# Mean sweeps of a graph network over 128 runs of the edge list, one run per partition

## The chip, the cores and the metric

One core of a Trainium2 chip runs the kernel; its engines are TensorE (PE), VectorE (DVE), ScalarE (ACT), GpSimd (POOL) and SyncE (SP). The metric is the device time of one execution in microseconds (us). Differences of up to 0.3% are about what a measurement of this kernel can't tell from none.

## The reference, cut to what matters

Four graph layers run over N = 6250 nodes of F = 128 features and E = 106250 edges (`src`, `dst`), which are sorted by `dst`. The last layer takes, twice, the mean of the neighbours' rows and two dense products:

```python
def _mean_aggregate(h, src, dst, num_nodes):
    msgs = h[src]
    summed = jax.ops.segment_sum(msgs, dst, num_segments=num_nodes)
    deg = jax.ops.segment_sum(jnp.ones((src.shape[0],), h.dtype), dst, num_segments=num_nodes)
    return summed / jnp.maximum(deg, 1.0)[:, None]

neigh = _mean_aggregate(x, src, dst, n)
h = jax.nn.relu(x @ W_in[0] + neigh @ W_in[1])
neigh = _mean_aggregate(h, src, dst, n)
return h @ W_out[0] + neigh @ W_out[1]
```

The three layers before it (a maximum over messages, a sum over messages, an attention) aren't touched. All is float32.

## The kernel before, in words

The program is a row of blocks, each with one instruction stream per engine; a block begins when all engines have ended the one before. A preparation block reads the edge list and makes tables: `src_cols` (the source node of each edge, 128 consecutive edges in a column of 128 partitions), marks that tell whether an edge has the same receiver as the one before it (written to memory, `edge_meta`), and for each node the row of its last edge (`end_i`) and one over its degree (`inv_deg`). Constants: T = 832 columns of P = 128 edges (106496 with padding), groups of CT = 4 columns (512 edges), NB = 208 groups, a ring of RING = 8 groups (32 columns), SLOTS = 4.

Stages 1 to 5 are each a sweep over the edges followed by a node phase in the same block. Stages 4 and 5 are the two mean aggregations; their sweep is `mean_phase` (from line 1306), written out without loops:

- POOL issues for each column an indirect DMA (L1321) that gathers 128 rows of 512 bytes of `sender_table`, one for each edge; before a group it waits on `e_pre` until the PE has transposed the group that used that place of the ring.
- The PE transposes the group (L1361), so that features lie on partitions and 512 edges along the row. VectorE runs a scan over them (L1404): sum = mark x sum + row, so a sum starts anew at each new receiver. The PE transposes back (L1371), ScalarE copies from PSUM (L1387), SP stores 256 KB to `scan_rows` (L1334) and counts stored groups in `e_kept`. SP also loads the marks, 1 MB for 8 groups, spread to all partitions (L1329).
- The row of a node's last edge in `scan_rows` then holds its sum.

The node phase (`node_phase`, from line 692) gathers on POOL those rows, 49 indirect DMAs in 13 groups of up to 4 (L746). Groups 0 to 3 wait only until the groups of edges that they need are stored, the others until all are. VectorE multiplies by `inv_deg` (L859), the PE transposes and multiplies (L1039 to L1057), ScalarE copies between (L978, L988), VectorE takes the result (L884), and SP stores it as the next stage's table (L779). The end of stage 4 is where the sweep of stage 5 begins; at the end of stage 5 a layer norm and the output follow. `scan_rows` is stored group-wise: 4 consecutive rows per partition (`"(p c) f -> p c f"`), which the preparation takes into account by permuting `end_i` (lines 611 to 618).

In the preparation, SP loads `dst` and `src` (L316 to L318), one word of each tile (L323), then the weights (L325, L341), and later stores `dst_rows` (L347), reads back each tile's last receiver (L353), after which VectorE counts (L557, L573) where each node begins. ScalarE meanwhile fills `receiver_rows` with zeros (L414), 2 MB each, in pieces of 16 KB that lie 832 rows of 512 bytes apart from partition to partition (line 404), and makes a factor table with the PE (L645, L655).

Of the kernel before, what the change touches and what calls it, by code (L numbers as in the profile page):

```python
# [17 lines left out]
P = 128  # L18
E = 106250
N = 6250  # L20
F = 128
# [19 lines left out]
assert NB % (2 * STRETCH) == 0 and STRETCH * CT * 4 == P  # L41
# [44 lines left out]
def gnn_program(nc, a, out):  # L86
# [14 lines left out]
    with ctx:  # L101
# [30 lines left out]
        end_i = sb("end_i", [P, NT], I32)  # L132
        mask = sb("mask", [P, NT])
# [114 lines left out]
        with ExitStack() as pctx:  # L248
# [23 lines left out]
            lasts, junk = carve("gath", [T]), (carve("gath", [T]), small[:, :, :].rearrange("p a b -> p (a b)")[:, 0:T])  # L272
            node_i = psb("node_i", [P, NT], I32)
# [35 lines left out]
            with nc.Block() as block:  # L309
                @block.sync  # L310
                def _(sp):

                    sp.wait_ge(filled, 3)
                    sp.sem_inc(filled, -3)
# [4 lines left out]
                    with nc.allow_non_contiguous_dma("one word of each tile"):  # L319
                        for c in range(TC):  # L320
                            lo, n = (1, P - 1) if c == 0 else (0, P if c < TC - 1 else rest + 1)
                            first = (c * P + lo - 1) * P
                            sp.dma_start(prev_r[lo:lo + n, c:c + 1],  # L323
                                         a["dst"][first:first + n * P].rearrange("(p k) -> p k", k=P)[:, P - 1:P]).then_inc(loaded, 16)
                    sp.dma_start(wm[:, :, :], a["L1_gnn_Wm"].rearrange("(t p) n -> p t n", p=P)).then_inc(wm_in, 16)  # L325
# [129 lines left out]
                def _(pool):  # L455
                    pool.memset(dst_r[:, TC - 1, :], N).then_inc(filled, 1)
                    pool.memset(src_r[:, TC - 1, :], 0).then_inc(filled, 1)
                    pool.memset(prev_r[:, 1:TC], N).then_inc(p_done, 1)
# [6 lines left out]
                    pool.wait_ge(p_done, 7)  # L465
                    pool.sem_inc(p_done, -7)
# [14 lines left out]
                def _(v):  # L481
# [58 lines left out]
                    chain(v.tensor_copy(head_ofT[:, :], bank[4][0:HEADS, 0:P]))  # L540
                    v.wait_ge(weights_in, 16 * 18)
# [62 lines left out]
                    chain(v.tensor_copy(end_i[:, :], end_f[:, :]))  # L604
                    chain(v.tensor_scalar(node_f[:, :], node_f[:, :], float(EP), None, ALU.add))
# [15 lines left out]
                def _(pe):  # L621
# [12 lines left out]
                    pe.transpose(bank[4][0:HEADS, 0:P], head_of[:, :], ident[:, :]).then_inc(turned, 1)  # L634

# [52 lines left out]
        marks = [over_head[:, :].bitcast(BF16)[:, h * RING * EB:(h + 1) * RING * EB] for h in range(2)]  # L688
# [3 lines left out]
        def node_phase(k):  # L692
# [35 lines left out]
            def gpsimd(pool):  # L728
                def gather(q, s):
                    g = 2 * q + s  # L730
                    if g == 0 or g - 1 in checked:
# [36 lines left out]
                if gathers:  # L768
# [537 lines left out]
        def mean_phase(k):  # L1306

            table, pre_ps, back_ps = send_d, bank[0:2], bank[4:6]
            before, rounds = started["edge"], NB // RING
            base, loads = NB * started["mean"], NB // RING  # L1310
            base_stored, base_marks = 16 * (NB // SLOTS) * started["mean"], 16 * (loads // 2) * started["mean"]

            def gpsimd(pool):
                for i in range(NB):
                    s = i % RING
                    if i >= RING:

                        pool.wait_ge(e_pre, base + i - RING + 1)
                    for c in range(CT):
                        t = i * CT + c  # L1320
                        pool.indirect_dma_start(out=gath[s][:, c, 0:F], out_offset=None, in_=table[:, :],  # L1321
                                                in_offset=bass.IndirectOffsetOnAxis(ap=src_cols[:, t:t + 1], axis=0)).then_inc(gathered[s], 16)

            def sync(sp):
                def load_marks(j):
                    if j >= 2:
# [603 lines left out]
```

## Time and profile before

| what | us |
|---|---|
| three executions | 7039.76, 7061.51, 7058.68 (median 7058.68) |
| profiled execution, its own time | 7064.64 |
| its span, first to last instruction | 7062.7 |
| its mean granted TensorE clock | 0.677 of full speed |

Times in the profile count from the first instruction. A group of instructions shows its busy time, the mean of one, and the idle time of its engine just before it with what ended it; "issue" is time in which the engine waited for nothing that the profile shows, "remote" an end that it can't name, and an engine's name with q is its sequencer. The windows show busy time and instruction count of each engine in a stretch.

### The profile page before, as it was taken

To read this page: it belongs to the slowest core of one execution; us is meant where nothing else is said; L and a number is where in the kernel's file an instruction comes from. 1 tells how busy PE (TensorE), PEld (TensorE's weight loads), DVE (VectorE), ACT (ScalarE), POOL (GpSimd) and SP (SyncE) were. 2 spreads that over 40 slices of the span, in tenths; PEclk is the share of its full clock that TensorE was granted. 3 is DMA by queue.
4 is the path that set the end of the run, shared out by engine and by line. 5 is a ranking of instruction groups with operands and counts; after the bars stand their busy time and mean duration, and the time that the engine had idled before them with its cause. 6 is when DMAs were issued, how large, how long until landed. Compare 5 with 4: busy or idle time off the path is not lost. (4 is left out here: it accounts for less than half of the span.)

```text
span 7062.7 us, 75749 instructions
## 1 busy us (share of the span) xinstructions
PE 3269.4 (46%) x16319; PEld 2442.7 (35%) x16319; DVE 2306.4 (33%) x4133; ACT 1222.9 (17%) x2253; POOL 3621.3 (51%) x3810
## 2 busy tenths in 40 slices
PE   1357777777647885344444443223222332222323
PEld 1334444444436663233333432122222222222222
DVE  4223333332346663233333335222222212222223
ACT  0111111111224442112112211011111111110111
POOL 2355555555440004655555553666666656666664
PEclk7667777777779997666666666555555565555556
DMA  9757767766448984222222222333333323333332
GB/s 266 234 173 223 218 206 214 217 207 211 139 139 295 317 292 99 67 76 78 77 78 77 79 75 68 98 115 117 117 109 116 113 72 116 117 116 115 112 122 73
DMA packets 701309, 1015.77 MB, mean 144 GB/s; under 512 B 151346, under 2 KB 403179, under 8 KB 691147
## 3 DMA queue, kind: packets, MB, share of 16 engines
q1 hardware_dynamic: 379672, 485.85, 21.5%
q0 software_dynamic: 134688, 301.60, 15.5%
q10 hardware_dynamic: 186780, 226.46, 9.4%
q8 instruction: 59, 0.97, 0.1%
q14 instruction: 110, 0.89, 0.0%
HBM read 580.89 MB, written 433.03 MB: 144 GB/s over the span
## 5 line engine op out<-in xcount | busy, mean ns | idle before, releaser
L1321 POOL DMA_INDIRECT gath<-sender_table,src_cols x1664 | 1571.3, 944 | 903.3 <-issue 488.2
L1361 PE MATMUL bank<-ident,gath 128*128 128x128 f32 x1664 | 405.4, 391 | 1739.2 <-issue 1192.5
L1404 DVE TENSOR_TENSOR_SCAN scan<-over_head,scan,bank 128x512 f32<-128x512 bf16 x416 | 532.2, 1279 | 1896.1 <-remote 1488.6
L1594 POOL DMA_INDIRECT gath<-attention_table,src_cols x832 | 796.2, 957 | 663.8 <-POOLq L1591 423.8
L1118 POOL DMA_INDIRECT gath<-joint_table,src_cols x832 | 788.2, 947 | 671.1 <-POOLq L1115 281.1
L1361 PEld LDWEIGHTS bank<-ident,gath 128*128 128x128 f32 x1664 | 278.1, 202 | 1842.0 <-issue 1783.3
L1387 ACT ACTIVATE rows<-bank 128x512 f32<-128x512 f32 x416 | 245.0, 597 | 2186.2 <-remote 1597.5
L1293 DVE TENSOR_TENSOR_SCAN scan<-meta,scan,bank 128x512 f32<-128x512 bf16 x208 | 266.1, 1279 | 835.2 <-DVEq L1290 434.4
L1857 DVE TENSOR_TENSOR_SCAN scan<-bank,scan,hid 128x512 f32<-128x512 f32 x208 | 266.6, 1282 | 643.5 <-DVEq L1856 339.7
L746 POOL DMA_INDIRECT gath<-scan_rows,end_i x147 | 140.0, 952 | 633.7 <-ACTq L1521 560.6
L1371 PE MATMUL bank<-ident,scan 128*128 128x128 f32 x1664 | 385.4, 377 | 1.5 <-DVE scan L1404 0.8
L1194 PE MATMUL bank<-hid,w 128*128 128x512 f32 x416 | 295.6, 802 | 126.7 <-PEq L1193 107.3
L1687 PE MATMUL bank<-ident,scan 128*128 128x128 f32 x832 | 175.8, 350 | 354.8 <-issue 191.0
L1186 PEld LDWEIGHTS bank<-same,recv 128*128 128x128 f32 x1664 | 256.6, 236 | 203.7 <-issue 203.7
L1371 PEld LDWEIGHTS bank<-ident,scan 128*128 128x128 f32 x1664 | 316.0, 205 | 2.4 <-DVE scan L1404 2.4
L1227 ACT ACTIVATE hid<-bank,b 128x512 f32<-128x512 f32 x208 | 143.0, 688 | 949.7 <-ACTq L1226 498.8
L1186 PE MATMUL bank<-same,recv 128*128 128x128 f32 x1664 | 303.7, 338 | 0.0
L1183 PE MATMUL bank<-ident,gath 128*128 128x128 f32 x832 | 166.6, 336 | 279.7 <-issue 142.1
L1184 PE MATMUL bank<-small,w1w 1*128 1x512 f32 x416 | 293.4, 791 | 0.0
L1679 PE MATMUL bank<-small,over_head 128*128 128x128 f32 x1664 | 285.6, 329 | 0.0
L1562 DVE TENSOR_TENSOR_SCAN scan<-bank,scan,hid 128x512 f32<-128x512 f32 x208 | 265.9, 1278 | 39.2 <-issue 14.8
L1679 PEld LDWEIGHTS bank<-small,over_head 128*128 128x128 f32 x1664 | 270.6, 246 | 0.0
(250 smaller groups left out, 5244.6 us busy)
## 6 DMA issues: line engine op xcount, KB each, us to landing
scan_rows<-rows SPq DMA_DIRECT2D x624, 256.0 KB
recv<-receiver_rows SPq DMA_DIRECT2D x416, 256.0 KB
attention_scan_rows<-rows ACTq DMA_DIRECT2D x208, 264.0 KB
receiver_rows<-gath ACTq DMA_DIRECT2D x26, 2048.0 KB
factor_rows<-gath ACTq DMA_DIRECT2D x208, 256.0 KB
scan_rows<-rows ACTq DMA_DIRECT2D x208, 256.0 KB
gath<-factor_rows SPq DMA_DIRECT2D x208, 256.0 KB
over_head<-edge_meta SPq DMA_DIRECT2D x52, 1024.0 KB
```

Of the source, the lines that this page charges most:

```text
L1118: pool.indirect_dma_start(out=landed[s][:, c, 0:width], out_offset=None, in_=table[:, :], in_offset=bass.IndirectOffsetOnAxis(ap=src_cols[ ...
L1184: pe.matmul(b[:, :], w1w[:, :], wrow[r][:, :], start=False, stop=False)
L1186: ins = pe.matmul(b[:, c * P:(c + 1) * P], recv[r][:, c, :], same[s % 2][:, c, :], start=False, stop=c == CT - 1)
L1194: pe.matmul(msg_ps[s % 2][:, :], w2[:, :], hid[s % 2][:, :], start=True, stop=True).then_inc(e_msg, 1)
L1293: chain(v.tensor_tensor_scan(scan[s % 2][:, :], go_on, src, scan[1 - s % 2][:, EB - 1:EB], ALU.add if expands else ALU.mult, ALU.max if ex ...
L1321: pool.indirect_dma_start(out=gath[s][:, c, 0:F], out_offset=None, in_=table[:, :], in_offset=bass.IndirectOffsetOnAxis(ap=src_cols[:, t:t ...
L1361: ins = pe.transpose(b[:, c * P:(c + 1) * P], gath[s][:, c, 0:F], ident[:, :])
L1371: ins = pe.transpose(back_ps[i % 2][:, c * P:(c + 1) * P], scan[i % 2][:, c * P:(c + 1) * P], ident[:, :])
L1404: v.tensor_tensor_scan(scan[i % 2][:, :], go_on, pre_ps[i % 2][:, :], scan[1 - i % 2][:, EB - 1:EB], ALU.mult, ALU.add).then_inc(e_scan, 1)
L1594: pool.indirect_dma_start(out=gath[s][:, c, :], out_offset=None, in_=att_d[:, :], in_offset=bass.IndirectOffsetOnAxis(ap=src_cols[:, t:t + ...
L1679: ins = pe.matmul(fac_ps[s % 2][:, c * P:(c + 1) * P], over_head[:, t * P:(t + 1) * P], factor_c[s // SB][:, :], start=True, stop=True)
L1857: chain(v.tensor_tensor_scan(scan[s % 2][:, :], fac_ps[s % 2][:, :], hid[s % 2][:, :], scan[1 - s % 2][:, EB - 1:EB], ALU.mult, ALU.add))
```

## The change

The edge list is cut into 128 runs of T = 832 consecutive edges, one per partition. Column t of the sweep is then edge t of each run, so that consecutive edges of a run follow each other in one partition, and the sums can be made row by row by VectorE, without transposes: `run_row(t)` = `run_row(t - 1)` x `goes_on[:, t]` + `run_row(t)`, in place in the ring, which has 4 slots of TR = 8 columns. SP stores a slot of 512 KB when it is summed, from each partition 4 KB that are consecutive in `scan_rows`. POOL, before it fills a slot again, waits for the slot's sums and its store.

A receiver whose edges cross the border of two runs is mended at the end: the last rows of all runs are transposed, scanned with `whole_row` (a run that is one single receiver passes its predecessor's sum on) and transposed back; POOL gathers for each run the row at which its first receiver ends (`lead_end`), VectorE adds what the runs before carry over, and POOL scatters the rows back. Only then does it gather for the nodes, all 49 without further waits, by `end_row`, which isn't permuted.

The preparation loads `src_run` and `dst_run` with two DMAs each, the last receiver of the run before each run (`before_run`, one word per partition) with one, and makes `goes_on`, `lead_end` and `whole_row` with some 20 more VectorE instructions and one matmul. ScalarE has nothing to do in the sweeps, and the marks aren't loaded there.

```diff
@@ preparation, SP, behind the loads of one word of each tile (POOL: three more fills and an iota ahead) @@
-                    sp.wait_ge(filled, 3)
+                    sp.wait_ge(filled, 6)
...
+                    runs = E // T
+                    for t, name in ((src_run, "src"), (dst_run, "dst")):
+                        sp.dma_start(t[0:runs, :], a[name][0:runs * T].rearrange("(p t) -> p t", t=T)).then_inc(run_loaded, 16)
+                        sp.dma_start(t[runs:runs + 1, 0:E - runs * T], a[name][runs * T:E].rearrange("(p t) -> p t", p=1)).then_inc(run_loaded, 16)
+                        sp.dma_start(before_run[1:P, :], a["dst"][0:(P - 1) * T].rearrange("(p t) -> p t", t=T)[:, T - 1:T]).then_inc(run_loaded, 16)
...
@@ preparation, VectorE, behind the copy to head_ofT @@
+                    v.wait_ge(run_loaded, 16 * 5)
+                    v.tensor_copy(lead_len[:, :], before_run[:, :]).then_inc(v_done, 1)
+                    v.tensor_copy(start_run[:, :], run_start[:, :]).then_inc(v_done, 1)
+                    v.tensor_copy(dst_flat[:, :], dst_run[:, :]).then_inc(v_done, 1)
+                    v.tensor_tensor(goes_on[:, 1:T], dst_flat[:, 1:T], dst_flat[:, 0:T - 1], ALU.is_equal).then_inc(v_done, 1)
+                    v.tensor_tensor(goes_on[:, 0:1], dst_flat[:, 0:1], lead_len[:, :], ALU.is_equal).then_inc(v_done, 1)
+                    chain(v.tensor_copy(goes_in[:, :], goes_on[:, :]))
+                    chain(v.memset(goes_in[:, 0:1], 1.0))
+                    chain(v.tensor_tensor_scan(dst_flat[:, :], goes_in[:, :], zero_c[:, 0:1].to_broadcast([P, T]), 1.0, ALU.mult, ALU.add))
+                    chain(v.reduce_sum(lead_len[:, :], dst_flat[:, :], mybir.AxisListType.X))
...
+                    v.tensor_copy(whole_all[:, :], lead_len[:, 0:1].to_broadcast([P, P])).then_inc(whole_ready, 1)
+                    v.wait_ge(whole_turned, 1)
+                    chain(v.tensor_copy(whole_row[:, :], bank[2][:, 0:P]))
...
+                    chain(v.tensor_copy(end_row[:, :], end_f[:, :]))
@@ preparation, PE, ahead of the factor table @@
+                    pe.wait_ge(whole_ready, 1)
+                    pe.matmul(bank[2][:, 0:P], whole_all[:, :], ident[:, :], start=True, stop=True).then_inc(whole_turned, 1)
@@ mean_phase, new bodies; all of the old ones goes @@
+            def gpsimd(pool):
+                for t in range(T):
+                    j = t // TR
+                    if t % TR == 0 and j >= SLOTS:
+                        pool.wait_ge(e_scan, summed_before + (j - SLOTS + 1) * TR)
+                        pool.wait_ge(stored[j % SLOTS], stored_before + 16 * (j // SLOTS))
+                    pool.indirect_dma_start(out=run_row(t), out_offset=None, in_=send_d[:, :],
+                                            in_offset=bass.IndirectOffsetOnAxis(ap=src_run[:, t:t + 1], axis=0)).then_inc(gathered[t // CT % RING], 16)
+                for s in range(SLOTS):
+                    pool.wait_ge(stored[s], stored_before + 16 * (RUNS // SLOTS))
+                pool.indirect_dma_start(out=lead_rows[:, :], out_offset=None, in_=scan_d[:, :],
+                                        in_offset=bass.IndirectOffsetOnAxis(ap=lead_end[:, :], axis=0)).then_inc(lead_in, 16)
+                pool.wait_ge(lead_summed, m + 1)
+                pool.indirect_dma_start(out=scan_d[:, :], out_offset=bass.IndirectOffsetOnAxis(ap=lead_end[:, :], axis=0),
+                                        in_=lead_rows[:, :], in_offset=None).then_inc(lead_out, 16)
+                pool.wait_ge(lead_out, 16 * (m + 1))
+            def sync(sp):
+                for j in range(RUNS):
+                    sp.wait_ge(e_scan, summed_before + (j + 1) * TR - 1)
+                    sp.dma_start(by_run[:, j * TR:(j + 1) * TR, :], run_rows[j % SLOTS]).then_inc(stored[j % SLOTS], 16)
+            def tensor(pe):
+                pe.wait_ge(e_scan, summed_before + T - 1)
+                pe.transpose(bank[0][:, 0:P], run_row(T - 1), ident[:, :]).then_inc(last_turned, 1)
+                pe.wait_ge(carries_made, m + 1)
+                pe.transpose(bank[1][:, 0:P], carries[:, 0:P], ident[:, :]).then_inc(carries_turned, 1)
+            def vector(v):
...
+                for t in range(T):
+                    if t % CT == 0:
+                        v.wait_ge(gathered[t // CT % RING], gathered_before + 16 * CT * (t // (CT * RING) + 1))
+                    if t > 1:
+                        v.wait_ge(e_scan, summed_before + t - 1)
+                    if t > 0:
+                        v.scalar_tensor_tensor(run_row(t), run_row(t - 1), goes_on[:, t:t + 1], run_row(t), ALU.mult, ALU.add).then_inc(e_scan, 1)
+                v.wait_ge(e_scan, summed_before + T - 1)
+                v.wait_ge(last_turned, m + 1)
+                v.tensor_tensor_scan(carries[:, 1:P + 1], whole_row[:, :], bank[0][:, 0:P], 0.0, ALU.mult, ALU.add).then_inc(carries_made, 1)
+                v.wait_ge(lead_in, 16 * (m + 1))
+                v.wait_ge(carries_turned, m + 1)
+                v.scalar_tensor_tensor(lead_rows[:, :], bank[1][:, 0:P], goes_on[:, 0:1], lead_rows[:, :], ALU.mult, ALU.add).then_inc(lead_summed, 1)
@@ node_phase, POOL @@
-                    if g == 0 or g - 1 in checked:
+                    if k <= 3 and (g == 0 or g - 1 in checked):
...
-                                                in_offset=bass.IndirectOffsetOnAxis(ap=end_i[:, t:t + 1], axis=0)).then_inc(node_got[g], 16)
+                                                in_offset=bass.IndirectOffsetOnAxis(ap=(end_i if k <= 3 else end_row)[:, t:t + 1], axis=0)).then_inc(node_got[g], 16)
```

## Rows read from the trace of the kernel before

**Rows 1.** The page: span, and two of its costliest groups
```profile
span 7062.7 us, 75749 instructions
...
L1321 POOL DMA_INDIRECT gath<-sender_table,src_cols x1664 | 1571.3, 944 | 903.3 <-issue 488.2
...
L1404 DVE TENSOR_TENSOR_SCAN scan<-over_head,scan,bank 128x512 f32<-128x512 bf16 x416 | 532.2, 1279 | 1896.1 <-remote 1488.6
```

**Rows 2.** Windows: preparation, sweep 4, its node phase, sweep 5, its node phase
```profile
core 0: us, PE busy (x) PEld busy (x) DVE busy (x) ACT busy (x) POOL busy (x), PEclk, DMA share, GB/s
0.00:262.60 262.60, 42.18 (x173) 35.01 (x173) 102.67 (x298) 15.83 (x27) 58.60 (x67) 0.71 0.94 274
...
4436.00:5616.40 1180.40, 334.95 (x1624) 284.23 (x1624) 258.44 (x202) 117.86 (x200) 785.62 (x832) 0.56 0.35 114
5616.40:5745.50 129.10, 54.21 (x239) 35.65 (x239) 24.75 (x32) 27.12 (x47) 46.81 (x50) 0.75 0.22 67
5745.50:6926.30 1180.80, 337.48 (x1624) 286.92 (x1624) 259.45 (x203) 118.18 (x201) 785.65 (x832) 0.56 0.35 114
6926.30:7062.70 136.40, 56.19 (x239) 35.94 (x239) 54.04 (x192) 21.92 (x46) 46.68 (x49) 0.71 0.21 64
```

**Rows 3.** Timeline where sweep 4 begins: start, duration, engine, line, idle before
```profile
4436.03 0.94 POOL L1321 DMA_INDIRECT gath<-sender_table,src_cols  x1 [61.29 <-POOLq L1867]
...
4439.78 0.94 POOL L1321 DMA_INDIRECT gath<-sender_table,src_cols  x1 [0.30 <-issue]
...
4443.51 0.90 PE L1361 MATMUL bank<-ident,gath 128*128 128x128 f32 x3 [9.60 <-DMA gath<-sender_table,src_cols]
```

**Rows 4.** Line L1321 alone: what ended POOL's idle time before it
```profile
  issue: 488.2, 1583
  remote: 251.1, 64
```

**Rows 5.** Timeline of a stall in sweep 4
```profile
4499.33 1.28 DVE L1404 TENSOR_TENSOR_SCAN scan<-over_head,scan,bank 128x512 f32<-128x512 bf16 x1 [21.15 <-remote]
...
4500.76 0.66 PE L1361 MATMUL bank<-ident,gath 128*128 128x128 f32 x2 [20.49 <-issue]
...
4510.77 0.94 POOL L1321 DMA_INDIRECT gath<-sender_table,src_cols  x1 [5.12 <-remote]
```

**Rows 6.** Groups by form, VectorE: the added operation, factor from SBUF, and without
```profile
L1841 DVE SCALAR_TENSOR_TENSOR small<-small,carried 128x128 f32<-128x128 f32 x26 | 9.1, 352 | 5.1 <-DVEq L1840 3.8 <-issue 1.1 <-DVE sum_carry L1838 0.2
...
L1812 DVE SCALAR_TENSOR_TENSOR small<-max_c,small 128x128 f32<-128x128 f32 x26 | 7.6, 292 | 3.9 <-issue 0.9 <-DVEq L1811 0.5
```

**Rows 7.** Timeline, node phase of stage 4: a gather begun under a VectorE instruction
```profile
5663.10 0.69 DVE L859 TENSOR_TENSOR recv<-gath,inv_deg 128x512 f32<-128x512 f32 x1 [0.44 <-DVE recv L884]
5663.25 1.36 POOL L746 DMA_INDIRECT gath<-scan_rows,end_i  x1 [0.30 <-issue]
```

**Rows 8.** Timeline, node phase of stage 4, from the last copy to the next sweep
```profile
5648.45 0.60 ACT L1387 ACTIVATE rows<-bank 128x512 f32<-128x512 f32 x1 [0.78 <-PE bank L1371]
...
5651.91 0.94 POOL L746 DMA_INDIRECT gath<-scan_rows,end_i  x1 [15.55 <-SPq L1339]
...
5692.39 0.95 POOL L746 DMA_INDIRECT gath<-scan_rows,end_i  x1 [0.30 <-issue]
5697.13 0.60 ACT L988 ACTIVATE hid<-bank 128x512 f32<-128x512 f32 x1 [25.27 <-ACTq L984]
...
5731.80 0.29 DVE L859 TENSOR_TENSOR recv<-gath,inv_deg 128x128 f32<-128x128 f32 x1 [0.44 <-DVEq L837]
...
5745.46 0.94 POOL L1321 DMA_INDIRECT gath<-sender_table,src_cols  x1 [52.12 <-POOLq L1867]
```

**Rows 9.** Timeline of the preparation: POOL's fill, SP's word-wise loads, VectorE's first count
```profile
1.28 3.51 POOL L462 MEMSET over_head<- 128x4096 f32 x1
...
16.86 13.44 SPq L323 DMA_DIRECT2D prev_r<-in_dst_dram  x7
...
86.12 1.08 DVE L557 TENSOR_SCALAR_CACHE_REDUCE gath<-gath,node_f 128x832 f32<-128x832 f32 x1 [30.09 <-DVEq L556]
```

More of the change, by code:

```diff
@@ L40 @@
 STRETCH = 8
-assert NB % (2 * STRETCH) == 0 and STRETCH * CT * 4 == P
+TR = 2 * CT
+RUNS = T // TR
+assert RUNS % SLOTS == 0 and T % TR == 0 and NB % (2 * STRETCH) == 0 and STRETCH * CT * 4 == P
 BIG = 3.0e38
@@ L132, in gnn_program @@
         end_i = sb("end_i", [P, NT], I32)
+        end_row = sb("end_row", [P, NT], I32)
+        src_run = sb("src_run", [P, T], I32); goes_on = sb("goes_on", [P, T])
+        whole_row = sb("whole_row", [P, P]); lead_end = sb("lead_end", [P, 1], I32)
         mask = sb("mask", [P, NT])
@@ L686, in gnn_program @@
         t_exp_p = sem("t_exp_p")
-        marks = [over_head[:, :].bitcast(BF16)[:, h * RING * EB:(h + 1) * RING * EB] for h in range(2)]
+        run_rows = [gath_flat[:, s * TR * F:(s + 1) * TR * F].rearrange("p (c f) -> p c f", f=F) for s in range(SLOTS)]
+        lead_rows, carries = prod[0][:, 0:F], prod[1][:, 0:P + 1]
+        lead_in, lead_out = rank_in
+        lead_summed, last_turned, carries_made, carries_turned = factor_out[0:4]
         started = {"node": 0, "scatter": 0, "firsts": 0, "edge": 0, "mean": 0}
@@ L767, in gpsimd @@
                                                 in_offset=bass.IndirectOffsetOnAxis(ap=first_dst[:, c:c + 1], axis=0)).then_inc(firsts_got, 16)
-                if gathers:
+                if 1 <= k <= 3:
                     pool.sem_inc(e_kept, -NB)
@@ L1306, in mean_phase @@
         def mean_phase(k):
[L1308 to L1311, printed above, removed]
-            def gpsimd(pool):
[L1314 to L1322, printed above, removed]
@@ L1324, in sync @@
-            def sync(sp):
-                def load_marks(j):
-                    if j >= 2:
-                        sp.wait_ge(e_scan, base + (j - 1) * RING)
-                    sp.dma_start(marks[j % 2], meta_d[0, j * RING * EB:(j + 1) * RING * EB].partition_broadcast(P)).then_inc(meta_in[j % 2], 16)
-                def store(i):
-                    sp.wait_ge(e_rows, base + i + 1)
-                    sp.dma_start(scan_d[i * EB:(i + 1) * EB, :].rearrange("(p c) f -> p c f", c=CT), rows_flat[i % SLOTS][:, :, :]).then_inc(stored[i % SLOTS], 16)
-                def kept(i):
-                    sp.wait_ge(stored[i % SLOTS], base_stored + 16 * (i // SLOTS + 1))
-                    sp.sem_inc(e_kept, 1)
-                load_marks(0)
-                load_marks(1)
-                for i in range(NB):
-                    store(i)
-                    if i >= 2:
-                        kept(i - 2)
-                    if i % RING == RING - 1 and i // RING + 2 < loads:
-                        load_marks(i // RING + 2)
-                kept(NB - 2)
-                kept(NB - 1)
@@ L1381, in scalar @@
[L1381 to L1404 removed]
+            m = started["mean"]
```

80 lines of the change are left out of this document (40 added, 40 removed).

## The prediction

> **What bounds the kernel now.** I read three things in order: the page for where the changed line stands, the windows by stage for how long each stage lasts, and the timeline inside a stage for what ends last there. The page puts POOL first by busy time at the mean sweeps' gather line, L1321, with VectorE's scan L1404 far behind it [rows 1]. In the windows the two sweeps last 1180.4 and 1180.8 us, and POOL works 785.6 us in each on its 832 gathers; PE, VectorE, ScalarE and the DMA engines (0.35) are all far from full [rows 2]. So one wants to know why 832 gathers take 1180 us. At the start of a sweep they go out 1.250 us apart (three gaps between 4436.03 and 4439.78), 0.94 of work and 0.30 until the next [rows 3]. 832 x 1.250 = 1040 us. The other 140 us a sweep are stalls: L1321's idle time splits into 488.2 us of those 0.30 gaps and 251.1 us ended by "remote" in only 64 places [rows 4].
>
> The stall can be seen in the timeline of the first sweep. Scan, copy and transposes stand still for some 21 us (VectorE 21.15, PE 20.49) while POOL goes on; POOL itself then waits 5.12 us at 4510.77 [rows 5]. It waits for `e_pre`, that is for the PE to have transposed the group that holds the ring's next place: 32 rows of 1.250 us are 40 us of cover, and the chain gather, transpose, scan, transpose back, copy eats it. It is not the gathered data that are late: a group's first transpose starts at 4443.51, 2.8 us after its last gather's issue ended at 4440.72 [rows 3]. I read the stall as the PE round trip's, since VectorE and ScalarE resume together and the PE after them. Why the PE is slow in answering, no row says.
>
> **The change, part by part.** *Sweeps, gathers.* They are as many, 832 a sweep, of the same form, so 1040 us is the floor and POOL remains the bound. What changes is who frees the ring. A slot of 8 rows is free when it is summed and stored; POOL asks at row 8j for slot j-4, whose last gather went out 25 gathers, 31 us, earlier. It needs: landing 2.8 us, sums 2 us, store. For a 256 KB store the rows give 2.9 us from the end of the last copy (5648.45 + 0.60) to POOL's start behind it [rows 8]; I take 4 for 512 KB, bounds 2.9 and 5.8. Together 9 us of 31. That its pieces lie 416 KB apart in memory is no cost that I can see: the preparation's zero fill has the same stride and the stage moves 274 GB/s [rows 2]. So both sweeps lose the stalls: 2 x 140.5 = **-281 us**. Removing the 52 loads of 1 MB marks, the 1664+1664 transposes and 416 copies is worth nothing by itself; they lie beside POOL.
>
> *Sweeps, VectorE.* 831 `scalar_tensor_tensor` of 128x128 replace 208 scans. Such an instruction with its factor read from SBUF takes 352 ns, without 292 [rows 6]. Each waits for the one before; with a tenth of a microsecond for that, 0.45 us a row against 1.250, so VectorE keeps up with a factor of 2.7. Its cost lies elsewhere: it holds up the gathers. At 5663.10 VectorE starts a two-operand instruction that ends at 5663.79, POOL starts a gather at 5663.25, and that gather takes 1.36 instead of 0.945 us [rows 7]: 0.41 more, the 0.54 us left of the other less 0.12. So a gather wants something 0.12 us after its start that such an instruction holds. The sums are active 4 x 0.352 of each 5 us, 28% of the time, and what is left of one when it is hit is 0.176 us on average: 0.05 us a gather, 41 a sweep, **+83 us**. Bounds: 0 if the bursts fall between the gathers' moments, and 0.175 us a gather (every second waits out a whole one), 291 us, if they fall on them. I take random phase, since landing times vary by tenths.
> By the Trainium skill (SBUF - State Buffer, Who interferes with whom) a VectorE instruction with two SBUF inputs contends with a GpSimd instruction that reads SBUF, as an exclusive lock that whoever comes first holds for its whole instruction. The gather's 0.41 us agrees in one direction; the other direction, a sum waiting out a gather, is rival 4.
>
> *Ends of the sweeps.* Before, from the last sweep gather's end (5616.4) to the next sweep's start are 129.1 us, and 136.3 to the end of the program [rows 2]. 16 of the 49 node gathers go at once, then POOL waits 15.55 us for the stores, and the last goes out at 5692.39 [rows 8]: 77 us after 5616.4. After: landing 2.8, four sums 1.8, store 4, lead gather 0.9+2.8, sum 0.4, scatter 1+2.8, so 16.5 us, then 49 x 1.250 = 61.2: 77.7 us. Even. The two transposes and the scan of carries (0.4 us at 128 columns) hide behind store and lead gather. What follows the last node gather may shrink: now it takes 52.1 us [rows 8], because ScalarE resumes only at 5697.13 after 25.27 us and eight groups of 4.7 us are still to do. Without such a pause the last group needs 2.8 + (5745.46 - 5731.80) = 16.5 us: 36 us less. These are the same instructions beside the same gathers, so I expect the pause again, a little milder as the PE comes rested: -8 each, bounds +2 and -36. **-16 us**.
>
> *Preparation.* SP gets five more DMAs ahead of the weights; the word-wise ones there cost 13.44/7 = 1.9 us each [rows 9]. Bounds 0 and 9.6, I take 5, plus 0.7 a table for POOL's fills ahead of the first load (3.51 us for 4096 columns, so 0.7 for 832). They delay `dst_rows` and so the counting. VectorE's some 20 new instructions (two of about 1.08 us like L557's of 832 columns, one scan near 2, the rest short, some 10 us with their waits) fit into its 30.09 us of idle time before 86.12 [rows 9]; without that cover they would cost the 10. PE's factor transposes wait for them too, ahead of fills that ScalarE issues; those wait for each other longer. The end rows' extra cast is 0.3. **+6 us**, bounds 0 and 20.
>
> **Sum** against the profiled execution's own 7064.64 us (span 7062.7, 2 around it): -281 + 83 - 16 + 6 = -208, thus 6857. The shown median is 7058.68, 6 below that execution: **6850 us**.
>
> **Rivals.** (1) *As summed*, chance 0.60; its own range is 6770 to 6930. (2) *The pauses behind the sweeps vanish too*, chance 0.12: -281 + 41 - 72 + 6 = -306, 6750. For it: a rested PE, and no scans queued. Against: the pause begins in the middle of the node stage, long after the sweep's work. (3) *The sums hit the gathers' moment often*, chance 0.13: a burst begins at a nearly fixed time after a landing, so phases can lock; at 0.13 us a gather, +216 instead of 83: 6985. Against: a group's burst of 1.8 us meets at most two gathers. (4) *Slower*, chance 0.09: sum and gather exclude each other as wholes. Then each gather waits out a sum: 0.94 + 0.30 + 0.35 = 1.60 us, 1331 us a sweep, +302 - 10 = 7350. It decides from 1.42 us a gather on, where 832 make today's 1180. For it: the gather at 5663.25, which came second and waited [rows 7]. Against: no row shows VectorE waiting; L1812's 26 hold 292 ns in a stage with gathers [rows 6]. (5) *It doesn't do what it says*, chance 0.06: the ring's stall is of slow landings, the stores' or gathers', and comes back at each 32 rows: 7050. Against it stands the 2.8 us of [rows 3] and a DMA share of 0.35.
>
> **How the numbers follow.** Within 0.3% (21 us) counts as no change, about what a measurement here can tell. Cases 1, 2, 3 make 0.85 faster; 5 is the 0.06 of the same; 4 the 0.09 of slower. The range goes from case 2's lower end to beyond case 3's centre: 6730 to 7000; outside lie cases 4 and 5 and a twentieth of the others.
>
> **What would show it.** Gathers 1.25 to 1.35 us apart with no long idle time in the sweeps; sweeps of 1040 to 1120 us; some gathers of 1.0 to 1.3 us, each begun under a sum; sums of 350 ns; 16 to 18 us between the last sweep gather and the first node gather; the first sweep starting 0 to 20 us later than 4436.03. It is wrong if POOL waits at row 8j for `stored` or `e_scan`, if a gather lasts above 1.1 us on average, or if sums last as long as gathers.

## The result and the profile after

The changed kernel takes 7094.76 us (median of 8 executions) against 7061.81 for the kernel before, run beside it on one chip (8): a ratio of 1.0054, 95% interval 1.0039 to 1.0068. It is slower by half a per cent; 6850 us were forecast, between 6730 and 7000.

The profiled execution took 7084.38 us against 7064.64, 19.7 more. The page, span and the two new groups:

```profile
span 7082.5 us, 68220 instructions
...
L1377 POOL DMA_INDIRECT gath<-sender_table,src_run x1664 | 1732.6, 1041 | 654.3 <-issue 541.8
...
L1426 DVE SCALAR_TENSOR_TENSOR gath<-gath,goes_on 128x128 f32<-128x128 f32 x1662 | 592.6, 357 | 1701.9 <-DVE gath L1426 728.0
```

The gathers last 1041 ns on average instead of 944 [rows 1], and the sums 357. The windows by stage, which answer to [rows 2]:

```profile
core 0: us, PE busy (x) PEld busy (x) DVE busy (x) ACT busy (x) POOL busy (x), PEclk, DMA share, GB/s
...
4499.60:5636.80 1137.20, 0.00 (x0) 0.00 (x0) 293.89 (x825) 0.00 (x0) 848.80 (x832) 0.50 0.31 95
5636.80:5787.70 150.90, 53.88 (x201) 32.34 (x201) 20.43 (x35) 22.33 (x39) 48.30 (x51) 0.66 0.17 48
5787.70:6924.90 1137.20, 0.00 (x0) 0.00 (x0) 293.84 (x824) 0.00 (x0) 883.75 (x832) 0.50 0.30 95
6924.90:7082.50 157.60, 53.40 (x201) 30.82 (x201) 50.84 (x195) 17.73 (x39) 48.32 (x51) 0.67 0.16 48
```

Three numbers make the 19.7. The sweeps fell from 1180.4 and 1180.8 to 1137.2 each: -86.8, where -198 were forecast. The stretches behind them grew from 129.1 and 136.4 to 150.9 and 157.6: +43.0, where -16 were. And the first mean sweep starts at 4499.60 instead of 4436.03: +63.6, of which 57.6 are there when POOL's first gather of the preparation goes out, at 161.50 instead of 103.86; +6 were forecast. (That gather moves between executions as well: the preparation of the kernel before, unchanged, gave 103.86 here and 116.82 in e11 below.)

**Inside a sweep** there are two paces. POOL alone, in windows of 100 us of sweep 4:

```profile
4500.00:4600.00 100.00, 75.83 (x80) 0.50 0.32 99
4600.00:4700.00 100.00, 75.68 (x80) 0.50 0.34 104
4700.00:4800.00 100.00, 74.93 (x75) 0.50 0.31 96
4800.00:4900.00 100.00, 74.11 (x73) 0.50 0.30 94
```

80 gathers in 100 us are the 1.25 us of [rows 3]. From some 190 gathers on it is 72 or 73, 1.40 us (0.15 us a gather for the last 640 is 96 of the 97 us by which the sweep misses 1040), and it stays there to the end. The timeline shows how differently the engines look in the two, first at the one pace, then at the other:

```profile
4651.71 0.95 POOL L1377 DMA_INDIRECT gath<-sender_table,src_run  x1 [0.30 <-issue]
4651.87 1.51 DVE L1426 SCALAR_TENSOR_TENSOR gath<-gath,goes_on 128x128 f32<-128x128 f32 x4 [3.41 <-DMA gath<-sender_table,src_run]
4652.96 0.95 POOL L1377 DMA_INDIRECT gath<-sender_table,src_run  x1 [0.30 <-issue]
...
4954.43 1.24 POOL L1377 DMA_INDIRECT gath<-sender_table,src_run  x1 [0.60 <-issue]
4954.99 0.35 DVE L1426 SCALAR_TENSOR_TENSOR gath<-gath,goes_on 128x128 f32<-128x128 f32 x1 [1.05 <-DVE gath L1426]
4955.97 1.10 POOL L1377 DMA_INDIRECT gath<-sender_table,src_run  x1 [0.30 <-issue]
4956.39 0.35 DVE L1426 SCALAR_TENSOR_TENSOR gath<-gath,goes_on 128x128 f32<-128x128 f32 x1 [1.05 <-DVE gath L1426]
```

At first four sums follow each other in 1.51 us, and the gather that begins under the last of them, at 4652.96, lasts 0.95 us as usual. Later each sum starts 1.05 us behind the end of the one before, for whose semaphore it waits, and gathers stretch. It looks like two engines in each other's way, rival 3 of the prediction. The experiments say that it is not.

**In the node phase of stage 4** (start, duration, engine, line, idle before; to be read against [rows 8]):

```profile
5670.01 2.05 PE L1111 MATMUL bank<-ident,hid 128*128 128x128 f32 x8 [1.00 <-issue]
...
5676.95 0.69 PE L1093 MATMUL bank<-ident,recv 128*128 128x128 f32 x4
...
5692.90 0.69 DVE L938 COPY recv<-bank 128x512 f32<-128x512 f32 x1 [20.93 <-remote]
...
5715.35 0.60 ACT L1032 ACTIVATE scan<-bank 128x512 f32<-128x512 f32 x1 [9.25 <-ACTq L1030]
...
5732.10 0.69 DVE L938 COPY recv<-bank 128x512 f32<-128x512 f32 x1 [37.37 <-DVEq L929]
...
5734.88 0.95 POOL L800 DMA_INDIRECT gath<-scan_rows,end_row  x1 [20.18 <-POOLq L797]
...
5787.74 0.95 POOL L1377 DMA_INDIRECT gath<-sender_table,src_run  x1 [51.91 <-POOLq L1897]
```

The PE has the first group's product by 5672.06, VectorE learns of it at 5692.90. The transposes of the third group are done by 5677.64, and ScalarE, free since 5706.10, copies them at 5715.35. Only from 5732.10 on do the groups follow each other again. POOL's 48th gather had ended at 5714.70; the 49th waits 20.18 us for its place in the node phase's own buffers, so that not all 49 go without further waits. Before, ScalarE resumed at 5697.13 [rows 8].

**In the preparation** SP's queue, which answers to [rows 9]:

```profile
35.81 25.46 SPq L337 DMA_DIRECT2D src_run<-in_src_dram  x1
61.32 0.84 SPq L336 DMA_DIRECT2D x_nm<-in_dst_dram  x1
62.20 15.05 SPq L337 DMA_DIRECT2D x_nm<-in_dst_dram  x1
77.29 0.59 SPq L339 DMA_DIRECT2D before_run<-in_dst_dram  x1
77.92 10.99 SPq L340 DMA_DIRECT2D wm<-in_L_gnn_Wm_dram  x1
...
97.57 0.38 SPq L362 DMA_DIRECT2D dst_rows<-gath  x1
```

From 34.73 (the first of the five) to 88.91 (the end of the first weights' wait behind them) the queue hardly moves; VectorE's first count comes at 143.75 instead of 86.12 [rows 9]. L337 and its like are small (586 words of one partition), but each stands behind a load of 127 partitions (L336). The DMA view of 62 to 77 us, in which the load of `dst` (412.8 KB in 127 partitions) runs almost alone, tells what those do:

```profile
DMA packets 121, 0.39 MB, mean 26 GB/s; under 512 B 3, under 2 KB 3, under 8 KB 121
...
q1 hardware_dynamic: 120, 0.39, 6.4%
```

26 GB/s and 6.4% of 16 engines: one of the 16 is at work (one alone would be 6.25%).

### The profile page after: what moved, and what is told of

The parts are those of the page before. It is cut to its first block and busy times, and to the rows that moved or that the text cites. A ratio compares the mean times of both kernels' runs of the same rounds, so it can differ in the third digit from the quotient of the medians.

```text
span 7082.5 us, 68220 instructions
## 1 busy us (share of the span) xinstructions
PE 2592.3 (37%) x12997; PEld 1856.6 (26%) x12997; DVE 2372.6 (33%) x5401; ACT 977.9 (14%) x1837; POOL 3795.5 (54%) x3818
## 5 line engine op out<-in xcount | busy, mean ns | idle before, releaser
L1377 POOL DMA_INDIRECT gath<-sender_table,src_run x1664 | 1732.6, 1041 | 654.3 <-issue 541.8
L1426 DVE SCALAR_TENSOR_TENSOR gath<-gath,goes_on 128x128 f32<-128x128 f32 x1662 | 592.6, 357 | 1701.9 <-DVE gath L1426 728.0
L1399 PE MATMUL bank<-ident,gath 128*128 128x128 f32 x2 | 1.0, 476 | 2298.8 <-DVE gath L1426 2298.8
L1399 PEld LDWEIGHTS bank<-ident,gath 128*128 128x128 f32 x2 | 0.4, 183 | 2299.2 <-DVE gath L1426 2299.2
L1032 ACT ACTIVATE scan<-bank 128x512 f32<-128x512 f32 (+1 forms) x52 | 29.8, 573 | 2404.7 <-issue 2341.6
L800 POOL DMA_INDIRECT gath<-scan_rows,end_i x49 | 46.6, 951 | 585.2 <-ACTq L1551 571.2
L1717 PE MATMUL bank<-ident,scan 128*128 128x128 f32 x832 | 170.8, 343 | 288.3 <-issue 184.6
L1237 PE MATMUL bank<-ident,gath 128*128 128x128 f32 x832 | 167.2, 337 | 278.7 <-issue 101.5
L1333 DVE TENSOR_SCALAR same<-rank,rank_cols 128x128 f32<-128x128 uint8 x832 | 186.4, 298 | 220.1 <-issue 108.7
L1499 PE MATMUL bank<-ident,gath 128*128 128x128 f32 x832 | 239.1, 287 | 8.0
```

The costliest lines, as they stand in the source:

```text
L1377: pool.indirect_dma_start(out=run_row(t), out_offset=None, in_=send_d[:, :], in_offset=bass.IndirectOffsetOnAxis(ap=src_run[:, t:t + 1], a ...
L1426: v.scalar_tensor_tensor(run_row(t), run_row(t - 1), goes_on[:, t:t + 1], run_row(t), ALU.mult, ALU.add).then_inc(e_scan, 1)
L1499: pe.matmul(o, factor[s][:, c, :], ident[:, :], start=True, stop=False, is_transpose=True)
```

## The experiments

Each profile is of one execution; ratios are to the kernel before on the same chip, with 95% intervals. The length of sweep 4 is that of its window, from its first gather to the end of its last.

### Whose are the sweep's 1.40 us, and whose the preparation's 58?

`e1_tables_late` moves the five loads behind SP's last store to `edge_meta` and the others, VectorE's chain ahead of its last count, and the PE's `whole_row` behind the factor table.

> The changed kernel with the runs' loads behind the last store of the preparation on SyncE's queue, VectorE's run-table chain ahead of its last count, and TensorE's transpose of it behind the factor table. Theory P (the five loads block SyncE's queue while the zero fills hold the DMA engines, and the stores of the sorted destinations stand behind them): the first gather of the preparation goes back from 161.5 us to 103 to 115, and the first sweep of the mean phases starts 45 to 60 us earlier than 4499.6; the whole is 45 to 60 us faster than the changed kernel. Rival Q (the preparation pays for the added bytes or for VectorE's work wherever they stand): less than 20 us come back.

Ratio 1.0011 (0.9989 to 1.0034). The first gather of the preparation came back, sweep 4 started at 4441.5:

```profile
102.32 1.11 POOL L496 DMA_INDIRECT xT<-dst_rows,tiles_i  x1 [90.45 <-POOLq L494]
```

So P holds for the first gather, 161.50 to 102.32, and for the sweep's start, 58 us earlier. For the whole it doesn't: by the two ratios to the kernel before, 1.0054 and 1.0011, e1 is about 30 us faster than the changed kernel, not 45 to 60. For the loads took their time in the new place too, 31.05 and 39.85 us of SP's queue at the two L379, and the node scatters began 190 us behind that gather, not 168.

`e2_no_sums`, `e3_one_input` and `e4_no_chain` change only VectorE's part of the sweep:

```diff
 e2: -  v.wait_ge(e_scan, summed_before + t - 1)
     -  v.scalar_tensor_tensor(run_row(t), run_row(t - 1), goes_on[:, t:t + 1], run_row(t), ...)
     +  if t % CT == CT - 1: v.sem_inc(e_scan, CT if t >= CT else CT - 1)
 e3: +  v.tensor_scalar(run_row(t), run_row(t), goes_on[:, t:t + 1], None, ALU.mult)
 e4: -  v.wait_ge(e_scan, summed_before + t - 1)
     +  v.scalar_tensor_tensor(run_row(t), run_row(t), goes_on[:, t:t + 1], run_row(t), ...)
```

> The changed kernel with the 831 sums of each sweep left out (the row sums are not computed; VectorE only passes on that rows have landed; gathers, stores and waits stay). Theory B (VectorE's sums and the gathers hold each other up: 1.367 us a gather instead of 1.250): both sweeps take 1040 to 1050 us instead of 1137, the whole is about 190 us faster. Theory A (the gathers can't keep 1.25 us for long by themselves, whatever VectorE does: after some 190 of them they go at 1.40): sweeps of 1120 to 1140 us, the whole within 20 us of the changed kernel.

> The changed kernel with each sum replaced by a scaling of the row in place (the previous row is not added): one tensor input from SBUF instead of two, the same waits and increments, each still waits for the one before. Theory B1 (it is the second input from SBUF that collides with the gathers): sweeps of 1040 to 1060 us and sums back to back. Theory C (it is the wait of each sum for the semaphore of the one before, which comes a microsecond late): sweeps still of 1120 to 1140 us and an idle time of about 1.05 us ahead of most operations. Theory A: as C in time, without that idle time mattering.

> The changed kernel with each sum made of the row and itself (the previous row is not added), so that no sum waits for the one before; two inputs from SBUF as before. Theory C: sweeps of 1040 to 1060 us. Theory B1: sweeps of 1120 to 1140 us, gathers longer than 1.0 us on average. Theory A: 1120 to 1140 us as well, with gathers of 0.95 us and idle time between them.

Ratios 1.0045 (1.0023 to 1.0066), 1.0052 (1.0033 to 1.0070) and 1.0036 (1.0014 to 1.0058). Sweep 4 took 1136.8, 1137.8 and 1137.1 us. Windows of e2, sweep 4 and two stretches of 100 us in it:

```profile
4526.30:5663.10 1136.80, 0.00 (x0) 0.00 (x0) 0.00 (x0) 0.00 (x0) 838.92 (x832) 0.50 0.29 96
...
4530.00:4630.00 100.00, 0.00 (x0) 0.00 (x0) 0.00 (x0) 0.00 (x0) 75.54 (x81) 0.50 0.32 105
5000.00:5100.00 100.00, 0.00 (x0) 0.00 (x0) 0.00 (x0) 0.00 (x0) 73.26 (x72) 0.50 0.28 94
```

With VectorE, PE and ScalarE doing nothing at all the sweep is as long, with the same two paces: B falls. B1 falls by e3, where one input is left and the sweep stays. C falls by e4, where no sum waits for another and the sweep stays; its late semaphores are there, but they are not the cause. A stands, except that it expected gathers of 0.95 us with idle time between them in e4: they lasted 1.062 us on average there, as they did with one input (1.063 in e3). What a gather lasts and what it idles share out the 1.40 differently from kernel to kernel. POOL is busy 838.92 / 832 = 1.008 us a gather here: of the 97 ns by which the changed kernel's gathers are longer than 944, 64 have nothing to do with sums.

What runs late is not the gathered rows. The end of sweep 4 in e4, at the slower pace:

```profile
5636.50 1.10 POOL L1377 DMA_INDIRECT gath<-sender_table,src_run  x1 [0.30 <-issue]
5639.15 1.14 DVE L1423 SCALAR_TENSOR_TENSOR gath<-gath,goes_on 128x128 f32<-128x128 f32 x4 [4.42 <-DMA gath<-sender_table,src_run]
...
5646.73 0.48 PE L1399 MATMUL bank<-ident,gath 128*128 128x128 f32 x1 [1148.37 <-remote]
```

The last gather ends at 5637.60 and its rows are summed 1.55 us later. The PE, which waits only for the last of these sums (over at 5640.29), begins 6.4 us behind it.

### What is 1.40 us made of?

`e5_no_stores` leaves out SP's stores (`sp.sem_inc(stored[...], 16)` in their place). `e6_half_bytes` and `e7_half_rows` are e2 with `run_row(t)[:, 0:F // 2]` from a table of 64-word rows, and with `run_row(t)[0:P // 2, :]`. `e8_paced` is the full changed kernel and adds, after every 24th gather,

```diff
+                    if t % 24 == 23:
+                        pool.memset(over_head[:, :], 0.0).then_inc(over_made, 1)
+                        pool.wait_ge(over_made, 1)
+                        pool.sem_inc(over_made, -1)
```

> The changed kernel without the 104 stores of 512 KB in each sweep (the summed rows are not written; SyncE counts them as written). The sweeps took 1137 us with and without sums, at 1.25 us a gather for the first 190 or so and 1.40 us after. Theory A1 (the gathers share the DMA engines with the stores, and that is what 1.40 is made of): sweeps of 1040 to 1060 us. Theory A2 (the limit is in the gathers alone): 1130 to 1140 us.

> The kernel of the second experiment (no sums) with each gather fetching 128 pieces of 256 bytes instead of 512. Theory A2b (the limit goes by bytes): sweeps of 1040 to 1050 us. Theory A2d (it goes by gathers or by their rows, one of each partition): 1130 to 1140 us as before.

> The kernel of the second experiment (no sums) with each gather fetching 64 rows of 512 bytes instead of 128 (partitions 0 to 63). If the limit goes by rows: it falls to some 0.70 us a gather, below what GpSimd takes to issue one, the sweeps take at most 1045 us and never change pace, and TensorE's answers in the node phases behind them come sooner (the time from the last node gather to the next sweep 52 to 60 us, not 73). If it goes by gathers: 1130 to 1140 us.

> The changed kernel in full, with a fill of 128 x 4096 words by GpSimd (3.5 us) behind every 24th gather of the mean sweeps, so that it asks for no more than one gather in 1.40 us. Theory A3 (a queue behind GpSimd serves a gather in 1.40 us and holds some 28 us of them; while it is full, the semaphores of the other engines come late): sweeps of 1165 to 1180 us, the sums back to back in all of them, and the queue is empty at their end, so that the time from the last node gather to the next sweep falls from 73 us to 50 to 56 and the 79 us at the end to 58 to 62; the whole within 30 us of the changed kernel. Rival (no queue; the late semaphores in the node phases come from TensorE having been idle for the sweep): those stay at 73 and 79 us, and the whole is 50 to 70 us slower than the changed kernel.

Sweep 4 took 1137.4 us without stores (DMA share 0.18 instead of 0.31), 1137.0 with half the bytes, 1136.6 with half the rows; the ratios were 1.0060, 1.0053 and 1.0058. A gather of 64 rows has a median of 903 ns against 945, so it is its being one instruction that costs, not its rows. Neither bytes, rows nor neighbours make the 1.40; it goes by gathers.

The first pace does change with the rows, and that tells what ends it. e7 up to its first late gather, and 140 us from there:

```profile
4517.60:4687.56 169.96, 0.00 (x0) 0.00 (x0) 0.00 (x0) 0.00 (x0) 126.93 (x141) 0.50 0.25 80
4687.56:4827.56 140.00, 0.00 (x0) 0.00 (x0) 0.00 (x0) 0.00 (x0) 100.02 (x101) 0.50 0.21 69
```

141 gathers go at 1.205 us and are then 141 x 0.195 = 27.5 us ahead of one in 1.40. In e2, with 128 rows, some 180 go at 1.248 us, 27 us ahead. So the pace drops neither with a number of gathers nor with a time, but with a lead of 27 to 28 us over one gather in 1.40.

e8 (ratio 1.0143, 1.0119 to 1.0168):

```profile
4531.60:5716.50 1184.90, 0.00 (x0) 0.00 (x0) 292.83 (x827) 0.00 (x0) 908.89 (x866) 0.50 0.29 92
5716.50:5850.70 134.20, 50.54 (x201) 30.53 (x201) 19.39 (x32) 22.34 (x39) 48.21 (x51) 0.69 0.19 54
```

34 fills of 3.5 us and their waits ask for 138 us more and the sweep grows by 48. The sums stay in bursts of four in 1.51 us even at 5604.15, 1070 us into the sweep, and no gather is longer than 1.072 us. The stretch behind shrinks from 150.9 to 134.2 and the last one from 157.6 to 140.9: 6 of the 17 us because the last sums are no longer late (12.2 us from sweep to node gathers, not 18.2), 11 from the node phase. I had expected 17 to 23 from the latter: from the 48th gather's end to the next sweep it was 62, not 50 to 56, and from there to the end of the program 68.5, not 58 to 62. VectorE still waited once for 40.2 us there. And the whole is some 63 us slower than the changed kernel (1.0143 against 1.0054), where A3 had said 30 and its rival 50 to 70: the sweeps came out at 1184.9, above A3's 1180, and the node phases gave back less. The rival's reason, that these stay at 73 and 79 us, is refuted; A3 is right on the sums and half right on the node phases.

### A queue, or a pace that drops for good?

`e9_one_pause` puts eight such fills behind gather 500 and none elsewhere. `e11_before_paced` puts one behind every 24th gather of the kernel before. `e10_loads_early` is e1 with the five loads alone back where the change had put them. `e12_weights_later` is e1 with the 18 loads of weights behind the stores of `dst_rows`.

> The changed kernel with one pause of GpSimd in each sweep, behind gather 500: eight fills of 128 x 4096 words, some 31 us together. Queue theory (one gather is served in 1.40 us, some 28 us of them can wait): the pause empties the queue, the next 190 gathers or so go at 1.25 us again, and a sweep takes 1137 to 1142 us as without the pause. Rival (the pace drops once, with what GpSimd has fetched or with time, and stays down): the pace behind the pause is 1.40 at once and a sweep takes about 1168 us.

> The kernel of the first experiment (run tables late) with the five loads of the runs back where the change had put them, ahead of the weights on SyncE's queue; VectorE's chain and TensorE's transpose stay late. If SyncE's queue is the cause of the lost 59 us: the first gather of the preparation at 145 to 162 us. If TensorE's factor table that stood behind the transpose (and so ScalarE's fills) is the cause: 103 to 115 us.

> The kernel before with a fill of 128 x 4096 words by GpSimd (3.5 us, 34 of them) behind every 24th gather of its mean sweeps. Queue theory (the 5.2 us pauses of its ring come from answers of TensorE that are late because gathers are asked for faster than 1.40 us each): with the fills the pauses vanish, a sweep takes 1180 to 1190 us as with the pauses, the whole within 20 us of the kernel before. Theory of my forecast (the pauses are the ring's own, from the order in which it is freed): fills and pauses add up, a sweep takes 1290 to 1320 us.

> The kernel of the first experiment (run tables late) and, on SyncE's queue, the 18 loads of the weights behind the stores of the sorted destinations instead of ahead of them. Each of those loads took 0.3 to 2.3 us of the queue before, 17 us together: the first gather of the preparation at 90 to 98 us instead of 102.3, the whole 5 to 12 us faster than the first experiment and 5 to 25 us faster than the kernel before. Rival: the stores then collide with the loads and nothing is gained.

e9, sweep 4 as a whole, a stretch ahead of the pause and one behind it:

```profile
4528.30:5672.40 1144.10, 0.00 (x0) 0.00 (x0) 292.32 (x825) 0.00 (x0) 866.79 (x840) 0.50 0.31 95
...
5100.00:5200.00 100.00, 0.00 (x0) 0.00 (x0) 25.30 (x71) 0.00 (x0) 74.09 (x72) 0.50 0.30 94
5246.60:5346.60 100.00, 0.00 (x0) 0.00 (x0) 28.43 (x80) 0.00 (x0) 75.62 (x81) 0.50 0.34 105
```

POOL paused for 34.1 us more than usual (35.35 between two starts) and the sweep grew by 6.9, to just above the 1137 to 1142 expected; sweep 5 took 1141.9 (ratio 1.0039, 1.0012 to 1.0066). The pace went from 72 back to 80 for about 190 gathers. So something serves a gather in 1.40 us and lets POOL run ahead by some 27 us; a pause up to that length is free. The queue theory stands as an account of the pace. What stands in that queue stays open: it isn't the rows, which land on time (e4).

e11 (ratio 1.0041, 1.0018 to 1.0063), the window of its sweep 4:

```profile
4467.40:5657.80 1190.40, 367.46 (x1648) 308.11 (x1648) 263.55 (x206) 121.30 (x204) 905.11 (x866) 0.53 0.37 114
```

POOL's idle time before L1321 in that sweep (what ended it: us, times):

```profile
  issue: 247.1, 790
...
  remote: 18.5, 14
```

And the same in sweep 4 of the kernel before:

```profile
  issue: 244.0, 791
...
  remote: 133.2, 35
```

120 us of fills cost 10 (1190.4, at the edge of the 1180 to 1190 expected; the whole 22 us longer by the medians), because the 133 us of "remote" in 35 places (both sweeps: [rows 4]) went down to 18.5 in 14. So the stalls of the kernel before come with asking faster than one in 1.40. They were more than that pace needs: 1180.4 us against 1137, so that of its 140 us a sweep 97 belong to the pace and 43 to the ring and its waits for the PE.

e10: ratio 1.0053 (1.0024 to 1.0082), first gather of the preparation at 173.50, later than the 145 to 162 expected and far from 103 to 115. So it is SP's queue, not the PE waiting for `whole_ready`. e12: ratio 1.0005 (0.9986 to 1.0025), first gather at 121.1, not 90 to 98, where the kernel before's own preparation, in e11, gave 116.8. Nothing is gained; that the stores collide with the loads, as the rival says, isn't shown.

### The shape of the loads

```diff
-                        sp.dma_start(t[0:runs, :], a[name][0:runs * T]...)
+                        for lo, hi in ((0, 112), (112, runs)):
+                            sp.dma_start(t[lo:hi, :], a[name][lo * T:hi * T]...)
```

and `before_run` likewise. `e13_loads_split` is the changed kernel with this alone, `e14_split_and_late` has e1 as well, `e15_split_chain_late` keeps the loads early and moves VectorE's chain and the PE's part.

> The changed kernel with the two loads of 127 partitions cut into 112 and 15 partitions each, and the load of one word of each run likewise; nothing else is moved. In the changed kernel's trace SyncE's queue moves 26 GB/s from 60 to 100 us, in packets of 3.3 KB that take 131 ns each, one at a time: the mark of a single DMA engine. Theory S (a load over 127 partitions runs on one DMA engine, one over 112 on 16): SyncE's queue is past the loads of the runs some 40 us earlier, the first gather of the preparation starts at 112 to 130 us instead of 161.5, and the first node scatter at 280 to 300 instead of 329.3. Rival (it is the bytes against the fills): no change in either, 155 to 165 us.

> The kernel of the first experiment (run tables late) with the loads cut as well. In the first experiment the loads took 71 us of SyncE's queue behind the other stores, and the first node scatter came at 292.8 us, 190 us behind the first gather of the preparation instead of 167. With theory S: 168 us behind it, at 268 to 280 us; the mean sweeps and their node phases give 44 us against the kernel before, so the whole is 25 to 45 us faster than the kernel before (ratio 0.994 to 0.9965). Rival: 290 us and more, ratio 0.998 to 1.003 as in the first experiment.

> The loads cut and in the place that the change gave them, ahead of the weights, with VectorE's chain and TensorE's transpose late. Theory S: like the kernel with loads cut alone or up to 10 us better, first gather of the preparation at 108 to 125 us; against the kernel before 15 to 40 us faster. Rival: first gather at 150 us and later as with the uncut loads there.

SP's queue in e13:

```profile
34.70 2.43 SPq L337 DMA_DIRECT2D src_run<-in_src_dram  x2
37.17 1.05 SPq L338 DMA_DIRECT2D src_run<-in_src_dram  x1
38.26 2.33 SPq L337 DMA_DIRECT2D x_nm<-in_dst_dram  x2
```

and its first gather of the preparation:

```profile
107.82 1.11 POOL L498 DMA_INDIRECT xT<-dst_rows,tiles_i  x1 [95.94 <-POOLq L496]
```

All eight loads are through by 44.37, at the same place, with the same bytes, against the same fills: 54 us of queue, the wait of the first weights behind them included, became 10. First gathers at 107.82, 116.20 and 128.7; ratios 0.9974 (0.9956 to 0.9992), 0.9973 (0.9955 to 0.9990) and 0.9993 (0.9977 to 1.0010). Theory S holds best where nothing else moved: e13's first gather came earlier than the 112 to 130 expected, its first node scatter at 278.3 (280 to 300). (The 26 GB/s that its expectation gives for 60 to 100 us end at 88.) In e14 the two pairs of loads take 1.37 and 1.05 us of SP's queue where e1's took 31.05 and 39.85, which is S again, but the scatter came at 291.1, 175 us behind the first gather and in the range of the rival; what else delays it is open. e15's first gather lies between S's 108 to 125 and the rival's 150, and its 5 us of gain, which its interval doesn't tell from none, miss the 15 to 40. e13 and e14 beat both kernels, by a quarter of a per cent against the one before; e14's forecast of 0.994 to 0.9965 was too good. The sweeps are 1137.2 us in them as well.

## Why the prediction was wrong, point by point

**The floor of 832 x 1.250 = 1040 us** is the step that failed worst: -281 should have been -87. It took three gaps at the start of a sweep for a pace that can be kept. It can for 190 gathers; then it is 1.40 whatever the other engines do (e2), so that the floor is 832 x 1.40 - 28 = 1137, and it is hit to within 1 us in all of e1 to e7. The kernel before hinted at it, had I divided: 1180.4 / 832 is 1.42, over a thousand microseconds. I took all of its stalls for the disease; 97 of the 140 us a sweep were how the limit showed itself (e11), and only the other 43 could be won and were: 2 x 43 is the 87. Rival 5 ("it doesn't do what it says") came closest, but it looked for the limit in landings, and rows land as fast at the slower pace (e4).

**The sums' contention, +83.** In the stretch where POOL isn't held by anything else, a gather lasts 75.83 / 80 = 0.948 us against 0.944 [rows 1]: 4 ns, not 50. In the rest it is hidden behind the 1.40. The phase was not what failed: in the first 200 us of sweep 4 a sum is running 0.12 us after the start of 54 of the 160 gathers, more than the 28% of the prediction. But these 54 last 0.969 us on average, the others 0.946; the longest is 1.08, and none waits out a sum with more than 0.14 us to go. The 0.41 us of [rows 7] was one gather under one instruction of another form, 128x512, and doesn't carry over; why, no run shows. The 1.041 us on average, which the prediction named as a sign of rival 3, was of another cause.

**The ends of the sweeps, -16; measured +43.** 18.2 and 18.8 us from the last sweep gather to the first node gather lie just above the 16 to 18 forecast, and only because the last sums came late: with sums on time it is 12.2 (e8). What follows is longer because POOL enters the node phase with the run-ahead used up: from the first gather of sweep 4 to VectorE's restart at 5732.10 are 1232.5 us, and 832 + 49 gathers of 1.40 are 1233. e1 and e13 repeat it with 1231.7 and 1232.5, and in e2, where the node gathers start 8 us earlier, it is 1229.8. The agreement argues for it; no run changes the lead alone. In e8 17 us of the 22 went. The rest stays open; one gap is known, the 15.55 us pause after 16 gathers that the kernel before makes [rows 8] and the changed one doesn't. Why the PE's answers are the late ones, by up to 38 us, while the PE takes up ScalarE's within 0.4 us (5706.10 to 5706.51), no run shows.

**The preparation, +6; measured +58, and 6 more on the way to sweep 4.** The term "five DMAs, at most 1.9 us each" was mis-sized: they are not small loads like `prev_r`. 127 partitions went through one DMA engine (6.4% of 16 while such a load ran, and e13). By the Trainium skill (DMA: Bandwidth & Descriptors, Why a DMA increments its semaphore by 16 and not by 1) a DMA runs on the largest number of engines up to 16 that divides the slowest dimension of both its sides; for 127 that is 1, for 112 it is 16. The trace agrees with its 26 GB/s at 6.4% of the 16 engines, and with e13. VectorE's chain and the PE's wait cost little where they stood, as forecast: with the loads cut the first gather comes 4 us later than before (107.82 against 103.86), and with chain and transpose moved away it did not come earlier (e15). As the same preparation gave 103.86 and 116.82, this can't be told more finely than by some 13 us.

**Right:** 350 ns a sum, the store and its slot in time (POOL's longest idle time in a sweep is 0.6 us, so it never waited long for `stored` or `e_scan`). Whether the removal of the transposes is worth nothing by itself, as the prediction says, no run shows: it went together with the ring, and the two gave 43 us a sweep. Stages that the change doesn't touch also differ between executions: the 832 gathers of stage 1 took 1453.7 us before, 1444.3 after and 1417.8 to 1481.5 in the experiments, so that medians move less cleanly than stages.

## What to carry to other kernels

Take the pace of a queue from its longest stretch, not from its first microseconds: divide the stage by its count, and if an engine stalls in a rhythm, ask whether the stall is a limit in disguise before pricing its removal. To find a limit's owner, take everything else out (one kernel without sums would have told before anything was built), then pause the suspect and see whether the pause costs its length. And count the partitions of each DMA: 112 + 15 took 10 us of queue where 127 took 54.

## What the runs showed of the hardware

- Indirect gathers from GpSimd: 1.25 us each for 180 to 190 in a row (1.205 for 141 with 64 rows instead of 128), then 1.40, with 128 or 64 rows, 512 or 256 bytes a row, with or without 512 KB stores beside them. The change of pace comes at a lead of 27 to 28 us. A pause of 34 us cost 7 and gave about 190 more their 1.25 back. The rows land 1.5 us behind the gather at the slower pace too.
- A gather of 64 rows has a median of 903 ns, one of 128 rows 945.
- While the gathers are held to 1.40, semaphores come late: a sum's by 1.05 us (0.04 before), the PE's by 21 to 38 us in the node phase.
- A load over 127 partitions moves 26 GB/s and holds what is behind it in its queue (25.46 and 15.05 us); cut at 112 the pair of loads takes 2.4.
